# An eight-stage kernel: the order of work in three of its stages (scales of an attention, ternary weight passes, output of a ternary FFN)

## The reference, cut to what matters

```python
def weight_quant(w):
    scale = jnp.clip(jnp.mean(jnp.abs(w), axis=-1, keepdims=True), 1e-05, None)
    quant = jnp.clip(jnp.round(w / scale), -1, 1) * scale
    ...
h = bitlinear(x, w1)      # 256 -> 1024
h = new_gelu(h)
return bitlinear(h, w2)   # 1024 -> 256
```

## Time and profile before

| | |
|---|---|
| median of 3 runs | 2503.26 us (2500.88 to 2507.92) |
| the profiled execution | 2503.51 us, span 2501.8 us |
| busy: PE, DVE, ACT, POOL | 82%, 72%, 61%, 37% of the span |
| preparation of the quantised attention | about 1267 to 1387 us of the span |
| causal attention | 2237 to 2398 us |
| SP's issue of the 18 DMA transposes of the ternary weights | 2338.83 to 2364.98 us |
| ternary FFN | 2398 to 2498 us |

### The profile page before, as it was taken

The page is one execution under the profiler, slowest core; times in us unless marked ns, Lnnn a source line. Parts: engine busy times, 40 slices in busy tenths (PEclk is TensorE's granted clock), DMA queues, the critical chain, the costliest instruction groups (busy, mean ns, idle before and its releaser), DMA issues. The chain is left out here.

```text
span 2501.8 us, 50609 instructions
## 1 busy us (share of the span) xinstructions
PE 2062.5 (82%) x17617; PEld 1136.3 (45%) x17617; DVE 1789.2 (72%) x3578; ACT 1514.2 (61%) x2762; POOL 930.3 (37%) x860
## 2 busy tenths in 40 slices
PE   4867999999987868999967688888888888568856
PEld 1344656565654644788634233333333332434433
DVE  5776755555555578433569899999999999566875
ACT  3454633333346755433325899999999999444565
POOL 5740000000003616000534577777777776224301
PEclk9778999999988979999978555555555555687989
DMA  6352211222223044122220354545455554110101
GB/s 200 83 218 71 69 64 67 67 67 67 67 84 98 3 175 158 40 69 65 80 89 1 64 93 90 93 89 93 91 92 93 90 93 90 17 68 2 29 1 34
DMA packets 384880, 195.41 MB, mean 78 GB/s; under 512 B 312301, under 2 KB 355311, under 8 KB 382703
## 3 DMA queue, kind: packets, MB, share of 16 engines
q1 hardware_dynamic: 381617, 184.47, 29.8%
q0 software_dynamic: 3072, 8.39, 1.0%
HBM read 94.99 MB, written 23.09 MB: 47 GB/s over the span
## 5 line engine op out<-in xcount | busy, mean ns | idle before, releaser
L2509 ACT ACTIVATE qa_e<-qa_S,qa_nb,qa_sq 128x512 uint8<-128x512 f32 (+1 forms) x805 | 708.8, 891 | 15.7 <-DVE qa_nb L2524 8.8
L2520 DVE TENSOR_REDUCE qa_mx<-qa_S 128x1 f32<-128x512 f32 x1024 | 636.9, 682 | 10.1 <-PE qa_S L2475 7.9
L2475 PE MATMUL qa_S<-qa_kT,qa_qb 128*128 128x512 f16 x1024 | 533.2, 608 | 117.0 <-ACT qa_e L2509 104.0
L2451 POOL CAST qa_pT<-qa_eT 128x2048 bf16<-128x2048 uint8 x256 | 483.5, 1891 | 209.8 <-DMA qa_eT<-qa_e 153.8
L2475 PEld LDWEIGHTS qa_S<-qa_kT,qa_qb 128*128 128x128 f16 x1024 | 89.6, 106 | 456.9 <-ACT qa_e L2509 440.9
L1116 POOL MEMSET rms_nothing<- 128x512 f16 x1 | 0.5, 524 | 579.8 <-POOLq L3508 579.8
L913 ACT ACTIVATE moe_ap<-moe_a 128x512 f16<-128x512 f32 x132 | 83.1, 630 | 194.4 <-DVE moe_a L935 194.4
L973 PE MATMUL moe_G<-hT,moe_W 128*128 (+1 forms) x792 | 193.8, 381 | 7.1 <-DVE moe_zero L941 7.1
L982 PE MATMUL moe_O<-moe_W,moe_ap 128*128 (+1 forms) x1584 | 194.5, 273 | 4.1 <-DVE moe_ap L937 4.1
L2484 PEld LDWEIGHTS qa_O<-qa_V,qa_pT 128*128 128x128 bf16 x4096 | 161.8, 107 | 74.1 <-issue 65.7
L973 PE MATMUL moe_U<-hT,moe_W 128*128 (+1 forms) x792 | 192.7, 380 | 0.0
(11 more groups left out here) (441 smaller groups left out, 3453.1 us busy)
## 6 DMA issues: line engine op xcount, KB each, us to landing
moe_wb<-weights_T SPq DMA_DIRECT2D x264, 128.0 KB, 2.8
moe_W<-in_moe_w SPq DMA_DIRECT2D x40, 384.0 KB, 11.7
moe_W<-in_moe_w SPq DMA_DIRECT2D x11, 1152.0 KB, 16.8
moe_xs_rows<-rms_nothing SPq DMA_DIRECT2D x46, 128.0 KB, 1.9
moe_ys_rows<-moe_ys SPq DMA_DIRECT2D x23, 256.0 KB, 2.1
conv_rows<-conv_parts SPq DMA_DIRECT2D x16, 256.0 KB, 3.0
qa_eT<-qa_e SPq DMA_TRANSPOSE x256, 3.0
conv_qst<-conv_rows SPq DMA_DIRECT2D x96, 32.0 KB
```

The costliest lines, as they stand in the source:

```text
L2451: nc.gpsimd.tensor_copy(pT[:, u % RING, :, :].rearrange("p (b r) q -> p b r q", r=2), pairs).then_inc(s_cast, 1)
L2475: nc.tensor.matmul(S[:, bank(m), :], qb[:, g // 2, j, g % 2, :], kT[:, g, q * QW:(q + 1) * QW], start=True, stop=True).then_inc(s_S, 1)
L2509: nc.scalar.activation(e8[:, u % RING, q * QW:(q + n) * QW], S[:, b:b + n, :].rearrange("p b c -> p (b c)"), ACT.Exp, bias=nb[:, u % 2:u % ...
L2520: nc.vector.reduce_max(mx[:, i, q:q + 1], S[:, bank(m + q), :], axis=AXX).then_inc(s_mx, 1)
```

## The change

Three edits, each only of order. In the quantised attention's preparation DVE's four `scales` no longer stand between the statistics but behind the key pairs 0 to 3. In the causal attention PE's `shifted_turned(t+1)` goes from before the last values to right behind `turned_back(t-1)`, ACT's copy of it between the two exponentials, and DVE's passes over the ternary weights are cut finer and lie in iterations 1 to 12. In the ternary FFN ACT's copy `turned(t-1)` stands behind GELU of t+1 and before the integers of t, PE's `down(t-1)` is written before `turned(t)` of the next turn of the loop (and so behind `integers_turned`), and DVE's output is that of tile t-2.

```diff
--- before.py
+++ after.py
@@ -2348,11 +2348,10 @@
 
                     for c in range(Q):
                         statistics(c)
-                        if c:
-                            scales(c - 1)
-                    scales(Q - 1)
                     for p in range(PAIRS):
                         keys(p)
+                        if p < Q:
+                            scales(p)
                     next_weights.start(dve)
                     low(0)
                     next_weights.magnitudes(dve, 0)
@@ -2885,18 +2884,21 @@
 
     def first_halves(self, dve):
         nc, chained = self.nc, self.chained
+        self.first_divided(dve, range(0, self.NF // 2))
         chained(nc.vector.tensor_copy(self.h16[:, :], self.s1[:, :]))
         chained(nc.vector.tensor_copy(self.h1[:, :], self.h16[:, :]))
         chained(nc.vector.tensor_tensor(self.l1[:, :], self.s1[:, :], self.h1[:, :], ALU.subtract))
-        for f in range(self.NF):
-            last = nc.vector.tensor_scalar(self.f1[:, f, :], self.f1[:, f, :], self.r1[:, f:f + 1], MAGIC, ALU.mult, ALU.add)
-        chained(last)
+
+    def first_divided(self, dve, rows):
+        for f in rows:
+            last = self.nc.vector.tensor_scalar(self.f1[:, f, :], self.f1[:, f, :], self.r1[:, f:f + 1], MAGIC, ALU.mult, ALU.add)
+        self.chained(last)
 
     def first_rounded(self, dve):
         self.chained(self.nc.vector.tensor_scalar(self.f1[:, :, :], self.f1[:, :, :], MAGIC, 1.0, ALU.subtract, ALU.min))
 
-    def first_scaled(self, dve, part):
-        for f in range(self.NF):
+    def first_scaled(self, dve, part, rows):
+        for f in rows:
             self.nc.vector.tensor_scalar(self.n1[:, part, f, :], self.f1[:, f, :], -1.0, (self.h1, self.l1)[part][:, f:f + 1],
                                          ALU.max, ALU.mult).then_inc(self.s_n1, 1)
 
@@ -2908,16 +2910,17 @@
         dve.wait_ge(self.s_s2, 1)
         chained(nc.vector.reciprocal(self.r2[:, :], self.s2[:, :]))
 
-    def second_rounded(self, dve):
+    def second_divided(self, dve):
         nc, chained = self.nc, self.chained
         for m in range(KT):
             last = nc.vector.tensor_scalar(self.f2[:, m, :], self.f2[:, m, :], self.r2[:, m:m + 1], MAGIC, ALU.mult, ALU.add)
         chained(last)
 
+    def second_rounded(self, dve):
+        self.chained(self.nc.vector.tensor_scalar(self.f2[:, :, :], self.f2[:, :, :], MAGIC, 1.0, ALU.subtract, ALU.min))
+
     def second_integers(self, dve):
-        nc, chained = self.nc, self.chained
-        chained(nc.vector.tensor_scalar(self.f2[:, :, :], self.f2[:, :, :], MAGIC, 1.0, ALU.subtract, ALU.min))
-        nc.vector.tensor_scalar(self.n2[:, :, :], self.f2[:, :, :], -1.0, None, ALU.max).then_inc(self.s_n2, 1)
+        self.nc.vector.tensor_scalar(self.n2[:, :, :], self.f2[:, :, :], -1.0, None, ALU.max).then_inc(self.s_n2, 1)
 
 
 def causal_attention(nc, sh, a, gate, next_weights):
@@ -3067,11 +3070,11 @@
                 shifted_queries(0)
                 for t in range(NB):
                     exponentials(t, 0)
+                    if t + 1 < NB:
+                        shifted_queries(t + 1)
                     if t + AHEAD < NB:
                         queries(t + AHEAD)
                     exponentials(t, 1)
-                    if t + 1 < NB:
-                        shifted_queries(t + 1)
                     if t + 5 < NB:
                         normalise(t + 5)
 
@@ -3150,14 +3153,18 @@
                     if t == 2:
                         next_weights.first_halves(dve)
                     if t == 3:
+                        next_weights.first_divided(dve, range(4, 8))
+                    if t == 4:
                         next_weights.first_rounded(dve)
-                    if t in (4, 5):
-                        next_weights.first_scaled(dve, t - 4)
-                    if t == 6:
+                    if 5 <= t < 9:
+                        next_weights.first_scaled(dve, (t - 5) // 2, range((t - 5) % 2 * 4, (t - 5) % 2 * 4 + 4))
+                    if t == 9:
                         next_weights.second_scales(dve)
-                    if t == 7:
+                    if t == 10:
+                        next_weights.second_divided(dve)
+                    if t == 11:
                         next_weights.second_rounded(dve)
-                    if t == 8:
+                    if t == 12:
                         next_weights.second_integers(dve)
                 output(NB - 1)
 
@@ -3246,6 +3253,8 @@
                     shifted_scores(t, 0)
                     if t:
                         turned_back(t - 1)
+                    if t + 1 < NB:
+                        shifted_turned(t + 1)
                     if t + AHEAD < NB:
                         queries_turned(t + AHEAD)
                     if t + SHIFTED < NB:
@@ -3256,8 +3265,6 @@
                     values(t, 0)
                     if t + SHIFTED < NB:
                         scores(t + SHIFTED, 1)
-                    if t + 1 < NB:
-                        shifted_turned(t + 1)
                     values(t, 1)
                 turned_back(NB - 1)
 
@@ -3362,12 +3369,14 @@
                 hidden(1)
                 integers_turned(1)
                 for t in range(NB):
+                    if t:
+                        down(t - 1)
                     turned(t)
                     if t + 2 < NB:
                         hidden(t + 2)
-                    down(t)
                     if t % Q == 1 and 1 < (t + 3) // Q < NQ:
                         integers_turned((t + 3) // Q)
+                down(NB - 1)
 
             @block.scalar
             def _(act):
@@ -3417,10 +3426,12 @@
                         tokens((t + 2) // Q)
                     if t + 1 < NB:
                         gelu(t + 1)
+                    if t:
+                        turned(t - 1)
                     integers(t)
                     if t + 10 < NB:
                         normalise(t + 10)
-                    turned(t)
+                turned(NB - 1)
 
             @block.vector
             def _(dve):
@@ -3490,12 +3501,13 @@
                     integers(t)
                 for t in range(NB):
                     rounded(t)
-                    if t:
-                        output(t - 1)
+                    if t >= 2:
+                        output(t - 2)
                     if t >= 2 and t + 6 < NB:
                         if t % Q == 2:
                             steps((t + 6) // Q)
                         integers(t + 6)
+                output(NB - 2)
                 output(NB - 1)
```

## The result

The changed kernel takes 2521.66 us (median of 6 runs, 2516.04 to 2532.3) against 2502.04 us for the kernel before (6 runs, 2498.34 to 2507.92): a ratio of 1.0079, 95% interval 1.0059 to 1.0100. It is slower by more than the 0.3% that counts as a difference here; 2517 was forecast. Its profiled execution took 2522.53 us, span 2520.8.

The account below looks back on a forecast made before the run. Eight barrier-closed stages in a row; DVE bounds the attention's preparation, two loops by turns the causal attention, a ring the ternary FFN. 2503.5 - 0.5 - 7 + 20.8 = 2516.8, say 2517 us; 8 in 10: 2504 to 2528.

Parts of the forecast that it names:

- Part 3: Ternary FFN: ACT's gT copy enters the ring (+9.0 us) and PE's clock falls (+11.8), together +20.8 us.
- part 2: Causal attention: finer, spread weight passes and earlier turning of the shifted queries, -7 us, bounds -11 and -3.
- Part 1: Quantised attention's preparation: scales behind key pairs, DVE held by POOL, -0.5 us, bounds -6 and +1.
- a light tile: Causal attention, iteration without a ternary weight pass: 7.58 us forecast against 7.26 before, 0.3 dearer.
- the larger of 7.58 and 5.53 + pass: Causal attention, iteration with a weight pass: period is the light one or DVE's time plus the pass.
- The tail's gain: End of causal attention, where no new scores come: two waits for the shifted queries go, about -0.8 us.
- The ring: Ternary FFN's chain of waits through the engines: 5.5 us a tile for 4.59, 6.87 with integers_turned; +9.0 us.
- Half: Ternary FFN: PE's clock falls in half of fourteen tiles, 7 x 1.68 = 11.8 us.
- The clock holds: Rival, 17%: PE keeps full clock in the ternary FFN, +9 there, 2505 us, no measurable change.
- It falls at every tile: Rival, 15%: PE's clock falls at every ternary FFN tile, +32.5 there, 2528 us.
- Faster by parts 1 and 2: Rival, 4%: DVE's short operations beat POOL's, -6 and -11 in the attention stages; 2495.5 us with clock held.
- best bound: Causal attention: -11 us if the copy of ca_O is no wait, 6.7 us for a light period.

Follow-up runs that it names:

- e6: Kernel before with attention's four scales inside key pairs 1 to 4, plus the causal-attention edits: 2483.86 us, one run (before: 2505.87).
- e7: Kernel before with only attention's four scales moved behind key pairs: 2502.31 us, one run (before: 2502.91).
- e4: Kernel before with the finer ternary weight passes alone: 2495.18 us, one run (before: 2505.87).
- e5: Kernel before with the earlier turning of the shifted queries alone, on PE and ACT: 2506.29 us, one run (before: 2505.87).
- e3: Changed kernel with eight needless PE matmuls in tiles 0 to 12 of the ternary FFN: ratio 1.0004 to the kernel before.
- e1: Changed kernel with the ternary FFN's old order on PE, ACT and DVE: ratio 0.9959 to the kernel before.
- e2: Changed kernel with only ACT's order in the ternary FFN put back: ratio 0.9963 to the kernel before.

## Why the prediction came out right, point by point

The sum was 2503.5 - 0.5 - 7 + 20.8 = 2516.8. The profiled execution gives 2503.5 + 0 - 9.8 + 31.0 - 2.2 = 2522.5. The direction, the order of the three parts by size and the mechanism of each held; the sizes were less good. Part 3's loss was 10.2 us too small. That the total is only 5.7 us off is luck: part 2 gained 2.8 us more than forecast, and code that the diff does not touch took 2.2 less, which hid half of it.

*Part 1* (-0.5, measured 0.0; the keys' end +0.5). The scale behind the pair was priced at 1.1 us and took 1.13. The first pair was not: I let it wait 1.3 us for the end of `qa_cT` and 0.9 for one subtraction, and it waited 3.5 for three POOL operations in a row. Before, the second and third were not ready in time: POOL waited 4.67 us for ACT's cast. I had left these where they were. But moving the scales let all statistics come at once, and ACT's casts with them, so they stood right behind `qa_cT`. It ended 20.5 us after the first statistics, for 19.6 forecast. That DVE waits for POOL, as the earlier trace rows show, is what made this part -0.5 and not -6. e6 confirms it by moving the instruction alone (0.16 us for 0.57), e7 that nothing was hidden. The Trainium skill ("SBUF — State Buffer", "Who interferes with whom") has it as a rule: a DVE instruction with two SBUF inputs contends with a GpSimd instruction that reads SBUF. The trace of e6 agrees.

*Part 2* (-7, measured -9.8). PE's wait for `ca_oT` was forecast at 0.9 us and is 0.68; a light tile 7.58, and is 7.40. The stretch from `ca_B` to the score half is the 4.34 us of the forecast (2360.13 to 2364.47); DVE's chain behind it is 0.18 shorter, as its negation takes 0.20 us for 0.38. From `ca_B(1)` to `ca_B(13)` 93.9 us were forecast and 90.7 measured: 1.3 us of it in the two tiles with the scales' passes (8.10 and 8.06 for 8.75). I took the pass at 3.2 us from the earlier trace rows, where one small operation in it took 0.67 us; here that takes 0.17, and the pass 2.75; the rest of the period is 5.35 us for 5.53. Another 1.1 us lie in the last period, which has no queries to turn (6.47, and 6.59 before), and 0.1 in each of eight others. The tail's gain was 0.66 for 0.8. I credited the turning with a loss of 0.3 and the passes with the rest; e4 and e5 show that the turning is worth 2.4 us of the 9.2 even with the short passes in place. The step that was incomplete is "the larger of 7.58 and 5.53 + pass": in the old order more stood behind the pass, ACT's copy and, at three of the waits, half clock.

*Part 3* (+20.8, measured +31.0). The ring came out to the hundredth: 5.50 us a tile, and 6.86 for the undisturbed step with integers (e3; 6.87 forecast), 79.7 us for fourteen steps and thus +9.0. The step that was mis-sized is the clock's. I took half of fourteen tiles, seven falls at 1.68 us, 11.8. There were eleven falls in fourteen tiles, one in every tile from the fourth on, and each cost 1.8 us, as the transposes and part of `down` are in the ring as well as hidden: 99.5 - 79.7 = 19.8 us. And the clock stayed low in the two tiles behind, where I had counted nothing: `down` takes 1.89 us for 1.05 and the transposes 1.06 for 0.62, and the 2.3 us by which the end is longer are these. (The waits for the last copies of `gT` there are 1.12 us in both kernels.) So the clock cost 22.1 us in all, not 11.8, with 9.0 for the ring. "Half" was a choice between two values, not worked out from rows. That PE's wait is the cause of the falls is what e3 shows: the falls go where the wait is filled, and come back in the one tile where it is not.

*The rivals.* "The clock holds" is excluded for the changed kernel and would have been right with PE fed (e3: ratio 1.0004, no measurable change, as that rival said). "It falls at every tile" was nearer in count than the forecast, but the gain of part 2 kept the total from 2528. "Faster by parts 1 and 2" did not come about: part 2 was near its best bound, though not by that rival's mechanism, as the copy of `ca_O` remained a wait, and part 1 was not.

## What to carry to other kernels

Before an operation is moved on one engine, write down the ring through all engines and ask whether something that lay beside it now lies in it: here one copy put 0.9 us into nearly every tile (9.0 us in all), and the wait that it made on PE cost more than twice as much again through the clock (22.1). The better order was one in which most operations depend on the other engines' step before and not on this one: 19 us gained in this stage where the change lost 31. Where DVE and POOL share a stretch, the place of a short DVE operation against POOL's start decides its price (0.16 or 0.57 us), and a change that makes one engine early can also pull forward the work of others and land DVE in front of a longer row of POOL work.

## What the runs showed of the hardware

PE's clock, in the ternary FFN: waits of 1.25 to 1.64 us in each tile of 4.6 to 5.5 us left it at 2.4 GHz (before, e1, e2, e3). It fell behind single waits of 2.12 and 2.16 (e3), 2.28 (e2) and 3.15 us (before, e1), but not behind each of them. With 2.12 us in each tile it stayed up for three tiles and then fell to 1.2 GHz in every one of eleven (changed kernel). In the causal attention it fell behind waits of 1.89 to 2.51 us (before, e5, e7), once stayed up behind one of 1.90 (e7), and never fell where the longest was 1.65 (e4). Adding eight needless matmuls (1.04 us) to each of thirteen tiles took 18.3 us off the stage.

A DVE `tensor_scalar` on 32 columns waited 3.5 us while POOL ran three operations back to back; it did not get in between them, in the changed kernel, e6 and e7 alike (3.71 us each time). DVE operations with an input in PSUM were never longer beside POOL: the reductions out of `qa_QP` took 0.68 to 0.69 us, the products with the reciprocals 0.69.
